# Subject-wise channel mixing with residual: stores and loads in turn in one DMA queue, 16 slots instead of 8

## The chip, the core and the metric

The kernel runs on one NeuronCore of a Trainium2 chip. The metric is the device time of one execution in microseconds (us); three runs of the kernel before lie between 334.43 and 335.13 us, with a median of 335.07 us. A difference of 0.2% is 0.67 us.

## What is computed

`x` is 128 samples of 128 channels by 1024 times, in float32 (67.1 MB). Each sample has a subject number from 0 to 7, and each subject a 128x128 weight matrix. The output is the sample plus its channels mixed by its subject's matrix:

```python
w = weights[subjects]                       # (128, 128, 128)
out = jnp.einsum('bct,bcd->bdt', x, w)      # one 128x128 by 128x1024 product per sample
x = x + out
```

Every byte of `x` is read once and every byte of the output is written once: 67.1 MB each way, and 0.5 MB of weights.

## The kernel before, in words

A tile is two samples (GROUP = 2): 128 partitions (channels) of 2 x 1024 floats, which is 1 MB. There are 64 tiles. They pass through `ring`, a buffer in SBUF with 8 slots (SLOTS) of one tile each; a turn is one pass over the slots, so there are 8 turns. The first turn and the last are written out, those between are a loop.

Each engine runs its own program, and semaphores tie them together:

- SyncE (SP) issues the loads, L82. From the second turn on it first waits, per slot, for the store that empties it (`stored[s]`, L76). The very last tile is loaded as two halves (L80).
- GpSimd (POOL) waits for the subject numbers and for the whole weight table (L91, L92). For each sample it reads the subject number (L97) and copies that subject's matrix from `table` to one of four buffers `selected` (L102).
- TensorE (PE) waits for the tile's load and for the selected matrix, and makes the product of the sample into one of four PSUM buffers (L126). The trace shows four matmul records for each sample, thus eight for a tile.
- VectorE (DVE) adds the product to the tile in its slot (L142) and counts `sum_ready`.
- ScalarE (ACT) computes nothing. It issues the loads of the subject numbers (L151) and of the table (L152), and then the stores: when both samples of a tile are summed it stores the tile (L168), the last tile in two halves (L163).

So loads travel in one DMA queue (SP's, q1 in the trace) and the table and all stores in another (ACT's, q10). Both queues are served by the same 16 DMA engines. What orders them is that a slot's load waits for the slot's store, and a store for the slot's sums.

Of the kernel before, what the change touches and what calls it, by code (L numbers as in the profile page):

```python
# [1 line left out]

# [5 lines left out]
I32 = mybir.dt.int32  # L24

GROUP = 2
SLOTS = 8
BUFS = 4
BANK = 512
DMA = 16  # L30


def subject_mix_kernel(nc: bass.Bass, x: bass.AP, subjects: bass.AP, weights: bass.AP, out: bass.AP):
    samples, channels, times = x.shape
    n_subjects, _, mixed = weights.shape
    per_turn = SLOTS * GROUP
    turns = samples // per_turn
    banks = times // BANK
    assert turns * per_turn == samples and banks * BANK == times and channels == mixed == 128
    assert per_turn % BUFS == 0  # L40
    uses = per_turn // BUFS


    x_view = x.rearrange("b c t -> c b t")
    out_view = out.rearrange("b d t -> d b t")

    with ExitStack() as ctx:
        def sem(name):
            return ctx.enter_context(nc.semaphore(name))

        ring = ctx.enter_context(nc.sbuf_tensor("ring", [channels, SLOTS, GROUP, times], F32))
        table = ctx.enter_context(nc.sbuf_tensor("table", [channels, n_subjects * mixed], F32))
        subject_row = ctx.enter_context(nc.sbuf_tensor("subject_row", [1, samples], I32))
        selected = ctx.enter_context(nc.sbuf_tensor("selected", [channels, BUFS, mixed], F32))
        products = ctx.enter_context(nc.psum_tensor("products", [mixed, BUFS, times], F32))


        subjects_loaded = sem("subjects_loaded")
        table_loaded = sem("table_loaded")
        x_loaded = [sem(f"x_loaded{s}") for s in range(SLOTS)]  # L60
        single_loaded = [sem(f"single_loaded{g}") for g in range(GROUP)]
        stored = [sem(f"stored{s}") for s in range(SLOTS)]
        weights_selected = sem("weights_selected")

        product_ready = [sem(f"product_ready{k}") for k in range(BUFS)]
        sum_ready = [sem(f"sum_ready{k}") for k in range(BUFS)]

        block = ctx.enter_context(nc.Block())

        @block.sync  # L70
        def _(sp):
            def go_round(turn, first=False, last=False):
                for s in range(SLOTS):
                    if not first:

                        sp.wait_ge(stored[s], turn * DMA)  # L76
                    start = turn * per_turn + s * GROUP
                    if last and s == SLOTS - 1:
                        for g in range(GROUP):
                            sp.dma_start(ring[:, s, g], x_view[:, start + g, :]).then_inc(single_loaded[g], DMA)  # L80
                        continue
                    sp.dma_start(ring[:, s], x_view[:, bass.ds(start, GROUP), :]).then_inc(x_loaded[s], DMA)  # L82

            go_round(0, first=True)
            with sp.Fori(1, turns - 1) as turn:
                go_round(turn)
            go_round(turns - 1, last=True)

        @block.gpsimd
        def _(pool):  # L90
            pool.wait_ge(subjects_loaded, DMA)  # L91
            pool.wait_ge(table_loaded, DMA)  # L92

            def go_round(turn, first=False):
                for j in range(per_turn):
                    k = j % BUFS
                    subject = pool.value_load(subject_row[0:1, bass.ds(turn * per_turn + j, 1)],  # L97
                                              min_val=0, max_val=n_subjects - 1)
                    if not first or j >= BUFS:

                        pool.wait_ge(product_ready[k], turn * uses + j // BUFS)
                    nc.gpsimd.tensor_copy(selected[:, k, :],  # L102
                                          table[:, bass.ds(subject * mixed, mixed)]).then_inc(weights_selected, 1)

            go_round(0, first=True)
            with pool.Fori(1, turns) as turn:
                go_round(turn)

        @block.tensor
        def _(pe):  # L110
            def go_round(turn, first=False, last=False):
                for j in range(per_turn):
                    s, g, k = j // GROUP, j % GROUP, j % BUFS

                    if last and s == SLOTS - 1:
                        pe.wait_ge(single_loaded[g], DMA)
                    elif g == 0:
                        pe.wait_ge(x_loaded[s], turn * DMA + DMA)

                    pe.wait_ge(weights_selected, turn * per_turn + j + 1)  # L120
                    if not first or j >= BUFS:

                        pe.wait_ge(sum_ready[k], turn * uses + j // BUFS)
                    for n in range(banks):
                        cols = slice(n * BANK, (n + 1) * BANK)
                        product = nc.tensor.matmul(products[:, k, cols], selected[:, k, :], ring[:, s, g, cols],  # L126
                                                   start=True, stop=True)
                    product.then_inc(product_ready[k], 1)

            go_round(0, first=True)  # L130
            with pe.Fori(1, turns - 1) as turn:
                go_round(turn)
            go_round(turns - 1, last=True)

        @block.vector
        def _(dve):
            def go_round(turn, first=False):
                for j in range(per_turn):
                    s, g, k = j // GROUP, j % GROUP, j % BUFS

                    dve.wait_ge(product_ready[k], turn * uses + j // BUFS + 1)
                    nc.vector.tensor_tensor(ring[:, s, g, :], products[:, k, :], ring[:, s, g, :],  # L142
                                            ALU.add).then_inc(sum_ready[k], 1)

            go_round(0, first=True)
            with dve.Fori(1, turns) as turn:
                go_round(turn)

        @block.scalar
        def _(act):  # L150
            act.dma_start(subject_row[:], subjects.rearrange("(a b) -> a b", a=1)).then_inc(subjects_loaded, DMA)  # L151
            act.dma_start(table[:].rearrange("c (n d) -> c n d", n=n_subjects),  # L152
                          weights.rearrange("n c d -> c n d")).then_inc(table_loaded, DMA)

            def go_round(turn, first=False, last=False):
                for s in range(SLOTS):
                    start = turn * per_turn + s * GROUP
                    if last and s == SLOTS - 1:
                        for g in range(GROUP):

                            j = s * GROUP + g
                            act.wait_ge(sum_ready[j % BUFS], turn * uses + j // BUFS + 1)
                            act.dma_start(out_view[:, start + g, :], ring[:, s, g]).then_inc(stored[s], DMA)  # L163
                        continue

                    for j in range(s * GROUP, (s + 1) * GROUP):
                        act.wait_ge(sum_ready[j % BUFS], turn * uses + j // BUFS + 1)  # L167
                    act.dma_start(out_view[:, bass.ds(start, GROUP), :], ring[:, s]).then_inc(stored[s], DMA)  # L168

            go_round(0, first=True)  # L170
            with act.Fori(1, turns - 1) as turn:
                go_round(turn)
            go_round(turns - 1, last=True)

            for s in range(SLOTS - 1):
                act.wait_ge(stored[s], turns * DMA)
            act.wait_ge(stored[SLOTS - 1], (turns - 1 + GROUP) * DMA)


# [14 lines left out]
```

## Time and profile before

| | |
|---|---|
| median of three runs | 335.07 us |
| lowest, highest | 334.43, 335.13 us |
| span of the profiled execution, first to last instruction | 330.9 us |
| rate over the span | 407 GB/s (134.78 MB) |
| PE busy | 234.2 us, 71% |
| DVE busy | 156.8 us, 47% |
| POOL busy | 37.8 us, 11% |
| granted TensorE clock, mean | 0.988 |

The span goes from the first to the last instruction of the program. The page gives no time of the profiled execution besides its span; the median of the runs is 4.2 us longer than the span (335.07 - 330.86), which is taken here for what lies around it. Busy shares are means over the whole span, and the first 60 us look different from the rest: there PE works without a pause.

### The profile page before, as it was taken

The page shows a single profiled execution, that of the slowest core. Times are in us where ns is not written, and L with a number is a line of the kernel's source. Part 1 is how long each engine was busy: PE and PEld are TensorE (multiplying, and loading weights), DVE is VectorE, ACT ScalarE, POOL GpSimd, SP SyncE. Part 2 cuts the span into 40 slices and gives each one's busy share as a digit, 9 for nine tenths or more (in the row PEclk, how much of TensorE's full clock was granted, in tenths as well). Part 3 has the DMA queues.
Part 4 walks back from the last instruction along what each step waited for, and adds up shares of the span by engine and source line. Part 5 has one row for each costly group of instructions (what it writes and reads, how often), then busy time and mean ns, then how long its engine had stood idle before and what let it go on. Part 6 is the DMA issues. An engine that isn't in the chain of part 4 may idle for free.

```text
span 330.9 us, 2706 instructions
## 1 busy us (share of the span) xinstructions
PE 234.2 (71%) x512; PEld 93.6 (28%) x512; DVE 156.8 (47%) x128; POOL 37.8 (11%) x133
## 2 busy tenths in 40 slices
PE   0069999976876866866866866866867767767750
PEld 0024444332332332322322322322322322322310
DVE  0017777745445445445445445445445445445450
POOL 0011111101111111111111111111111111111000
PEclk9999999999999999999999999999999999999995
DMA  7996999999999999999999999999999999999997
GB/s 272 391 409 245 364 420 419 419 421 423 420 420 420 420 421 421 421 422 420 420 420 420 421 422 422 420 420 420 419 421 421 423 421 420 420 420 421 421 421 308
DMA packets 35893, 134.78 MB, mean 407 GB/s; under 512 B 2097, under 2 KB 3122, under 8 KB 35890
## 3 DMA queue, kind: packets, MB, share of 16 engines
q10 hardware_dynamic: 18466, 67.64, 50.3%
q1 hardware_dynamic: 17424, 67.11, 50.0%
q8 instruction: 1, 0.02, 0.0%
q14 instruction: 2, 0.02, 0.0%
HBM read 67.63 MB, written 67.11 MB: 407 GB/s over the span
## 4 chain that ended last, share of the span: by engine, by line
DMA 75%; PE 17%; DVE 3%; issue 1%; ACTq 0%; POOLq 0%; SPq 0%; POOL 0%
DMA out<-ring 46%; DMA ring<-x 24%; PE products L126 17%; DMA table<-weights 5%; DVE ring L142 3%; POOLq L97 0%; ACTq L151 0%; ACTq L168 0%; SPq L82 0%; ACTq L167 0%; POOLq L102 0%; POOLq L92 0%; POOL selected L102 0%
## 5 line engine op out<-in xcount | busy, mean ns | idle before, releaser
L126 PE MATMUL products<-ring,selected 128*128 128x512 f32 x512 | 234.2, 604 | 84.6 <-DMA ring<-x 65.1
L142 DVE TENSOR_TENSOR ring<-products,ring 128x1024 f32<-128x1024 f32 x128 | 156.8, 1225 | 163.2 <-PE products L126 163.2
L126 PEld LDWEIGHTS products<-ring,selected 128*128 128x128 f32 x512 | 93.6, 191 | 224.3 <-issue 162.5
L102 POOL COPY selected<-table 128x128 f32 x128 | 37.6, 294 | 272.7 <-PE products L126 253.0
L185 POOL MEMSET const-float32-0.0<- 128x1 f32 x1 | 0.1, 98 | 0.1
L185 POOL MEMSET const-bfloat16-1.0<- 128x1 bf16 x1 | 0.1, 101 | 0.0
L185 POOL MEMSET const-uint8-127<- 128x1 uint8 x1 | 0.1, 101 | 0.0
L185 POOL MEMSET const-float32-1.0<- 128x1 f32 x1 | 0.1, 98 | 0.0
L185 POOL BASE_LOAD x1 | 0.0, 17 | 0.2 <-issue 0.2
## 6 DMA issues: line engine op xcount, KB each, us to landing
ring<-x SPq DMA_DIRECT2D x63, 1024.0 KB, 11.4
out<-ring ACTq DMA_DIRECT2D x63, 1024.0 KB, 22.9
ring<-x SPq DMA_DIRECT2D x2, 512.0 KB, 10.7
out<-ring ACTq DMA_DIRECT2D x2, 512.0 KB, 10.3
table<-weights ACTq DMA_DIRECT2D x1, 512.0 KB, 16.7
subject_row<-subjects ACTq DMA_DIRECT2D x1, 0.5 KB
```

What stands on the lines that cost most here:

```text
L102: nc.gpsimd.tensor_copy(selected[:, k, :], table[:, bass.ds(subject * mixed, mixed)]).then_inc(weights_selected, 1)
L126: product = nc.tensor.matmul(products[:, k, cols], selected[:, k, :], ring[:, s, g, cols], start=True, stop=True)
L142: nc.vector.tensor_tensor(ring[:, s, g, :], products[:, k, :], ring[:, s, g, :], ALU.add).then_inc(sum_ready[k], 1)
L185: nc = bacc.Bacc("TRN2", target_bir_lowering=False, num_devices=1)
```

## The change

All data transfers but the 0.5 KB of subject numbers are now issued by SP, in one queue. SP issues the table first, then loads of the first eight tiles. From there on it takes turns: it waits until tile t is summed, issues the store of tile t, waits (from tile 8 on) until the store of tile t-8 has landed, whose slot it needs, and issues the load of tile t+8. The ring has 16 slots, so there are 4 turns of 16. The last tile is loaded and stored whole. ACT issues the subject numbers and nothing else. What PE, DVE and POOL do with a tile stays as it was.

```diff
-SLOTS = 8
+SLOTS = 16
+AHEAD = 8
...
         @block.sync
         def _(sp):
+            def load(tile, s):
+                sp.dma_start(ring[:, s], x_view[:, bass.ds(tile * GROUP, GROUP), :]).then_inc(x_loaded[s], DMA)
+
+            sp.dma_start(table[:].rearrange("c (n d) -> c n d", n=n_subjects),
+                         weights.rearrange("n c d -> c n d")).then_inc(table_loaded, DMA)
+            for tile in range(AHEAD):
+                load(tile, tile)
+
             def go_round(turn, first=False, last=False):
                 for s in range(SLOTS):
-                    if not first:
+                    tile = turn * SLOTS + s
+                    for j in range(s * GROUP, (s + 1) * GROUP):
+                        sp.wait_ge(sum_ready[j % BUFS], turn * uses + j // BUFS + 1)
+                    sp.dma_start(out_view[:, bass.ds(tile * GROUP, GROUP), :], ring[:, s]).then_inc(stored[s], DMA)
+                    if last and s >= SLOTS - AHEAD:
+                        continue
+                    into = (s + AHEAD) % SLOTS
+                    if s >= SLOTS - AHEAD:
 
-                        sp.wait_ge(stored[s], turn * DMA)
-                    start = turn * per_turn + s * GROUP
-                    if last and s == SLOTS - 1:
-                        for g in range(GROUP):
-                            sp.dma_start(ring[:, s, g], x_view[:, start + g, :]).then_inc(single_loaded[g], DMA)
-                        continue
-                    sp.dma_start(ring[:, s], x_view[:, bass.ds(start, GROUP), :]).then_inc(x_loaded[s], DMA)
+                        sp.wait_ge(stored[into], turn * DMA + DMA)
+                    elif not first:
+                        sp.wait_ge(stored[into], turn * DMA)
+                    sp.dma_start(ring[:, into], x_view[:, bass.ds((tile + AHEAD) * GROUP, GROUP), :]
+                                 ).then_inc(x_loaded[into], DMA)
...
         @block.scalar
         def _(act):
             act.dma_start(subject_row[:], subjects.rearrange("(a b) -> a b", a=1)).then_inc(subjects_loaded, DMA)
-            act.dma_start(table[:].rearrange("c (n d) -> c n d", n=n_subjects),
-                          weights.rearrange("n c d -> c n d")).then_inc(table_loaded, DMA)
-
-            def go_round(turn, first=False, last=False):
...
```

At the head of the program, SP before: eight loads, and in the loop a load for each slot behind the wait for its store (`stored0` is slot 0's).

```order
L82 DMA ring<-x 128x2x1024 x8
L85 UNCONDITIONAL_BRANCH
L85 ISA
L82 ISA [waits stored0]
L82 DMA ring<-x 128x2x1024
L82 ISA [waits stored1]
L82 DMA ring<-x 128x2x1024
```

At the same place ACT before: the table, then the stores, each behind the two sums of its tile.

```order
L149 UNCONDITIONAL_BRANCH [waits barrier_Pool_Activation_PE_DVE_SP_release]
L151 DMA subject_row<-subjects 1x128
L152 DMA table<-weights 128x8x128
L168 DMA out<-ring 128x2x1024 [waits sum_ready1,sum_ready0]
L168 DMA out<-ring 128x2x1024 [waits sum_ready3,sum_ready2]
```

SP now, at the head of the program and where the first slots are used again:

```order
L59 DMA table<-weights 128x8x128
L57 DMA ring<-x 128x2x1024 x8
L69 DMA out<-ring 128x2x1024 [waits sum_ready1,sum_ready0]
L78 DMA ring<-x 128x2x1024
L69 DMA out<-ring 128x2x1024 [waits sum_ready3,sum_ready2]
L78 DMA ring<-x 128x2x1024
...
L69 DMA out<-ring 128x2x1024 [waits sum_ready1,sum_ready0]
L78 DMA ring<-x 128x2x1024 [waits stored0]
```

The table has moved from ACT to the front of SP, and each store has come between two loads; the first eight of those loads wait for no store. At the end of the program SP before (above) and now (below):

```order
L82 DMA ring<-x 128x2x1024 [waits stored5]
L82 DMA ring<-x 128x2x1024 [waits stored6]
L80 DMA ring<-x 128x1024 [waits stored7]
L80 DMA ring<-x 128x1024
L47 UNCONDITIONAL_BRANCH
```

```order
L69 DMA out<-ring 128x2x1024 [waits sum_ready1,sum_ready0]
L78 DMA ring<-x 128x2x1024 [waits stored14]
L69 DMA out<-ring 128x2x1024 [waits sum_ready3,sum_ready2]
L78 DMA ring<-x 128x2x1024 [waits stored15]
L69 DMA out<-ring 128x2x1024 [waits sum_ready1,sum_ready0]
L69 DMA out<-ring 128x2x1024 [waits sum_ready3,sum_ready2]
```

Behind the last load there now stand eight stores in the same queue (the last two rows, four times over).

## Rows read from the trace of the kernel before

**Rows 1.** The page: span, busy time, 40 slices of the span.
```profile
span 330.9 us, 2706 instructions
PE 234.2 (71%) x512; PEld 93.6 (28%) x512; DVE 156.8 (47%) x128; POOL 37.8 (11%) x133
DMA  7996999999999999999999999999999999999997
GB/s 272 391 409 245 364 420 419 419 421 423 420 420 420 420 421 421 421 422 420 420 420 420 421 422 422 420 420 420 419 421 421 423 421 420 420 420 421 421 421 308
```
**Rows 2.** Windows: start:end and us, busy us of each engine, PEclk, DMA share, GB/s.
```profile
0.00:3.00 3.00, 0.00 (x0) 0.00 (x0) 0.00 (x0) 0.22 (x5) 1.00 0.28 30
6.00:17.00 11.00, 0.00 (x0) 0.00 (x0) 0.00 (x0) 0.00 (x0) 1.00 1.04 394
18.00:24.00 6.00, 4.51 (x7) 2.08 (x8) 0.97 (x1) 1.46 (x5) 1.00 1.03 412
25.00:27.00 2.00, 2.00 (x6) 0.93 (x5) 1.51 (x2) 0.46 (x2) 1.00 0.05 18
29.00:31.00 2.00, 2.00 (x6) 0.80 (x6) 1.51 (x2) 0.29 (x1) 1.00 0.60 240
31.00:34.00 3.00, 3.00 (x9) 1.33 (x8) 2.01 (x3) 0.59 (x2) 1.00 0.99 288
34.00:37.00 3.00, 3.00 (x9) 1.33 (x8) 2.02 (x3) 0.33 (x2) 1.00 1.01 332
42.00:60.00 18.00, 18.00 (x43) 7.98 (x42) 13.07 (x11) 3.23 (x11) 1.00 1.03 421
60.00:300.00 240.00, 178.78 (x390) 69.84 (x388) 119.12 (x98) 28.51 (x97) 1.00 1.02 421
317.00:328.00 11.00, 1.73 (x4) 0.42 (x3) 2.45 (x2) 0.00 (x0) 0.77 1.02 419
328.00:331.00 3.00, 0.00 (x0) 0.00 (x0) 0.00 (x0) 0.00 (x0) 0.50 0.23 92
```
**Rows 3.** The chain that ended last, in order of time: start, us, what.
```profile
1.38 16.66 DMA table<-weights
...
72.30 3.71 PE products L126 x8
...
76.04 1.23 DVE ring L142
...
77.48 22.84 DMA out<-ring
...
100.48 11.35 DMA ring<-x
```
**Rows 4.** Timeline around the first tiles: start, us, engine, line, what.
```profile
19.49 25.82 PE L126 MATMUL products<-ring,selected 128*128 128x512 f32 x56 [19.49 <-POOL selected L102]
...
26.06 17.54 ACTq L168 DMA_DIRECT2D out<-ring  x6
```
**Rows 5.** DMA queues from 18 to 24 us, packets, MB, share of 16 engines.
```profile
q1 hardware_dynamic: 635, 2.47, 103.1%
```
**Rows 6.** DMA queues from 317 to 328 us.
```profile
q10 hardware_dynamic: 1206, 4.61, 102.1%
```
**Rows 7.** DMA queues from 6 to 17 us.
```profile
q10 hardware_dynamic: 982, 0.50, 15.7%
```
**Rows 8.** DMA queues from 31 to 34 us, and from 34 to 37 us below.
```profile
q10 hardware_dynamic: 206, 0.79, 93.7%
q1 hardware_dynamic: 17, 0.07, 5.6%
...
q1 hardware_dynamic: 240, 0.96, 98.0%
q10 hardware_dynamic: 13, 0.04, 3.0%
```
**Rows 9.** Line 82, SP's loads: ns to issue, min/median/max; then times to landing.
```profile
L82 SPq DMA_DIRECT2D ring<-x x63: 367/373/2648, 0.8 to 299.6; - x63
...
DMA to landing us min/median/max: 5.3/11.4/20.3
```

29 lines of the change are left out of this document (5 added, 24 removed).

## The prediction, made before the changed kernel ran

> **What bounds the kernel now.** I read the page's slices first. The DMA row stands at 9 in all but a few slices, and the rate is flat at 420 GB/s from slice 6 to slice 39, while PE is busy for 71% and DVE for 47% of the span [rows 1]. So the data transfers bound the kernel, and its time is the bytes by the rate plus the stretches in which the rate is not reached. The windows give those [rows 2]. The flat rate is 421 GB/s (60 to 300 us, DMA share 1.02), and at that rate the page's 134.78 MB take 320.1 us. The span is 330.9 us, so 10.8 us are lost. A window loses its length times (1 - rate/421):
>
> - 0 to 3 us, start: 3 x (1 - 30/421) = 2.8 us
> - 6 to 17 us, the table's small packets among the loads: 11 x (1 - 394/421) = 0.7 us
> - 25 to 27 us, almost no transfer (18 GB/s): 1.9 us
> - 29 to 31 us (240 GB/s, share 0.60): 0.9 us
> - 31 to 34 and 34 to 37 us (288 and 332 GB/s, but share 0.99 and 1.01): 0.95 + 0.63 = 1.6 us
> - 328 to 331 us, the end: 2.3 us
>
> That is 10.2 of the 10.8 us; the rest is spread thinly over 18 to 24 us (412 GB/s) and windows I don't list. The chain and the timeline say why 25 to 31 us are lost. The table needs 16.66 us to land because it shares the engines with eight loads [rows 3]; PE can't start before 19.49 us, and the first store leaves at 26.06 us [rows 4]. By then all eight slots have been loaded, and no load can be issued until a store has emptied one. Behind that, PE makes tiles at 8 x 0.43 = 3.43 us each, so stores alone don't fill the engines. Later PE has a tile only every 5 us and is no limit.
>
> **The change, part by part.** The sum goes against this execution: a span of 330.9 us and 4.2 us around it, which makes 335.1, the median.
>
> 1. *Table first.* The table no longer shares the engines with loads. Its 982 packets between 6 and 17 us took 15.7% of 16 engines for 11 us, which is 28 ns each [rows 7]. All 1024 alone: 64 on each engine, 1.8 us, where 0.52 MB at 421 GB/s take 1.25 us. The loss is then 0.55 us against 0.7 us before: no change. That these packets take 28 ns with no large packet among them isn't shown by any row. The upper bound is the time of a 4 KB packet, 4096 B at 421/16 GB/s = 156 ns, which would make it 10 us and cost 8.2 us. I take 28 ns, the only row with such packets.
>
> 2. *The gap from 25 to 31 us goes: -2.8 us.* With the table landed at about 5 us and the first load 2.5 us behind it, PE starts at about 8.5 us. The first store left 6.57 us after PE's start (26.06 - 19.49) [rows 4], so now at about 15 us. The table and eight loads keep the queue busy until 2.8 + 1.8 + 8 x 2.5 = 24.6 us. The first store and ninth load stand in the queue almost 10 us before they are needed, and the ninth load waits for no store, as there are 16 slots. From there PE yields a pair of work (store and load, 5 us) every 3.43 us, so the queue grows.
>
> 3. *The slow stretch from 31 to 37 us: -1.6 us.* Here the engines were not idle; packets took longer. First q10 moves nearly everything (93.7% of the engines), then q1 (98.0%) [rows 8], although the other queue also had transfers issued: it is the first meeting of a queue of stores and a queue of loads. With one queue there is no such meeting. Bounds: all 1.6 us go, or all stay. I take it as gone, since the stretch comes once, and 42 to 60 us run at 421.
>
> 4. *One queue instead of two: +1.5 us.* In the flat stretch packets of two queues take turns. A queue alone appears twice: stores alone from 317 to 328 us at 419 GB/s (1206 packets, all q10) and loads alone from 18 to 24 us at 412 GB/s (all q1) [rows 2, 5, 6]. At 419 the 134.78 MB take 321.7 us, 1.5 us more than at 421. I use this for loads too: a load burst is now 1 MB long (2.5 us), with stores on both sides. The bounds are 421 (0 us) and 412 for the loads; the latter adds 67.1 MB x (1/0.412 - 1/0.419) = 2.7 us (GB/s written in MB per us).
>
> 5. *SP's waits.* SP now waits for the sums of tile t, and behind that wait stands the load of t+8. From the landing of load t it takes 0.2 + 3.71 + 1.23 = 5.2 us until both samples are summed [rows 3]. Between load t and store t the queue holds 14 transfers, 35 us of work, so SP comes 30 us early. If the queue takes only about 8 transfers (before, with eight loads issued, one issue took 2648 ns against a median of 373 [rows 9]), SP is held by the queue and not by the sums, with about 12 us to spare still. The added wait for store t-8 is for a transfer that stands directly ahead of load t and has long landed. Two issues cost 0.75 us of each 5 us. All this costs nothing; the cover is the queue's backlog. ACT waits no more and nobody waited for it otherwise.
>
> 6. *The end.* Before, the last tile came in halves, and the engines ran at 419 until 328 us. Now eight stores stand behind the last load, 20 us of work, against 5.2 us for the last sums. The last store goes without a gap. The end's 2.3 us stay. PE's idle time before the end costs nothing.
>
> Sum: 330.9 - 2.8 - 1.6 + 1.5 = 328.0 us of span, and with 4.2 us around it **332.2 us**, 0.9% less than before.
>
> **The rivals.**
>
> *A. Loads in bursts run at the load-only rate.* Nothing else changes, the loads run at 412 GB/s: 332.2 + 2.7 = 334.9 us, no change. For it: the six-microsecond stretch of loads alone, the only long one in the trace. Against it: with one queue the engines need not be in step, some may store while others load. I give it one in six. The Trainium skill ("DMA: Bandwidth & Descriptors", section "iDMA fabric — 4 AXI ports for 8 engines, asymmetric across TPBs") has a load stream issued from SP, in 1 MiB transfers of 4 KiB rows and with nothing beside it, at 408.7 GB/s; an estimate from that page's figure is 4.0 us above my sum, 336.2 us. By that rule, the trace agrees within 1% in its stretch of loads alone (412 GB/s), and shows no stretch of loads in bursts between stores.
>
> *B. Each change of direction costs.* In one ring a load stands behind a store and has to read from HBM while the store's writes drain. From the first store to the last load there are 113 changes of direction. The gain of my sum, 2.9 us, is used up if each costs 26 ns, a sixth of a packet's 156 ns. For it: when stores and loads first met, an engine's packets took up to half as long again (288 against 421 GB/s at a full share) [rows 2, 8], which lost 1.6 us over two or three changes; at that price for all, some 0.5 us each, the kernel would take 390 us. Against it: in the flat stretch each engine has both directions under way at all times at 421 GB/s, but with a queue for each. Priced at one packet for each of the 56 loads behind a store, 56 x 0.156 = 8.7 us: 340.9 us, slower. A price of a third of that gives 335.1 us.
>
> *C. The rate doesn't fall.* If the 419 of stores alone is only the unevenness of the end, item 4 is nothing and the time is 330.7 us, or 330.1 if the small losses between 17 and 42 us that I don't list go as well.
>
> *D. The table is slow alone.* At twice to three times 28 ns, the added cost is 1.8 to 3.6 us, which puts it at 334 to 336 us. That the change doesn't do what it says (SP held at a wait while the queue runs dry) I give almost nothing, since the cover in item 5 is more than twice the need.
>
> **How the numbers follow.** A measurement of this kernel tells about 0.2% (0.67 us) from no change, so faster is below 334.4 and slower above 335.7. My forecast with C on its lower side, 330.0 to 334: 0.55. Rival A, 334 to 335.6: 0.17. Rival D: 0.06, half of it within 0.2%. Rival B: 0.22, of which half lies below 339. The predicted time is the forecast's, 332.2. The range 330.0 to 339.0 leaves out about 0.11 above and less than 0.05 below. Faster: 0.55 + 0.03 + a part of A = 0.60; same: 0.16; slower: 0.24.
>
> **What would show it.** In the changed kernel's profile: q1 carries nearly all bytes; PE starts near 8.5 us and the first store is issued near 15 us (item 2); no window between 20 and 45 us falls below 410 GB/s (items 2, 3); the rate from 60 to 300 us is 419 (item 4; 416 for A, 421 for C, 410 or less for B); loads take over 30 us to land and nobody waits for them longer; the table lands at about 5 us (8 or later for D); the last window looks as before. I am wrong if the flat rate is below 415, or if SP waits for sums while the DMA share drops.

## The result: 5.5 us faster, below the predicted range

The changed kernel takes 329.21 us (median of four runs, 328.76 to 329.42), the kernel before 334.75 us with one more run added to its three. The ratio is 0.984, with a 95% interval from 0.982 to 0.987. The prediction said 332.2 us and a range from 330.0: the direction was right, the gain was nearly twice the forecast, and the time lies 0.8 us under the range.

The page of the changed kernel, the lines that answer to [rows 1]; in the 40 slices the dip near slice 4 is gone:

```profile
span 327.7 us, 2553 instructions
DMA  7999999999999999999999999999999999999995
GB/s 259 410 409 419 422 420 420 419 421 421 420 422 420 421 419 421 420 420 422 421 422 420 421 422 421 421 422 421 422 421 420 422 421 420 422 421 421 422 420 243
...
q1 hardware_dynamic: 35856, 134.75, 100.6%
```

Its windows, against [rows 2] (start:end and us, busy us of each engine, PEclk, DMA share, GB/s):

```profile
3.00:6.00 3.00, 0.00 (x0) 0.00 (x0) 0.00 (x0) 0.00 (x0) 1.00 1.09 375
6.00:17.00 11.00, 9.24 (x16) 4.10 (x17) 3.67 (x3) 2.05 (x7) 1.00 1.03 411
...
25.00:27.00 2.00, 2.00 (x6) 0.84 (x5) 1.51 (x2) 0.29 (x1) 1.00 1.01 416
27.00:29.00 2.00, 2.00 (x6) 0.95 (x5) 1.40 (x2) 0.29 (x1) 1.00 1.03 418
29.00:31.00 2.00, 2.00 (x6) 0.86 (x5) 1.23 (x1) 0.29 (x1) 1.00 1.03 420
31.00:34.00 3.00, 3.00 (x9) 1.33 (x8) 2.41 (x2) 0.59 (x2) 1.00 1.02 419
34.00:37.00 3.00, 3.00 (x9) 1.33 (x8) 2.02 (x3) 0.59 (x2) 1.00 1.03 423
...
60.00:300.00 240.00, 176.29 (x384) 69.06 (x384) 117.26 (x96) 28.15 (x96) 1.00 1.02 421
...
317.00:325.00 8.00, 0.00 (x0) 0.00 (x0) 0.00 (x0) 0.00 (x0) 0.50 0.90 371
325.00:328.00 3.00, 0.00 (x0) 0.00 (x0) 0.00 (x0) 0.00 (x0) 0.50 0.06 23
```

Three things are to be seen. From 25 to 37 us the rate never falls below 416 GB/s, where before four of the five windows had 18, 240, 288 and 332. The flat stretch runs at 421 GB/s with one queue, exactly as with two. And the end is worse than before: from 317 us on the engines thin out.

The timeline of the first tile (start, us, engine, line, what), against [rows 4]:

```profile
7.76 8.71 PE L123 MATMUL products<-ring,selected 128*128 128x512 f32 x14 [7.76 <-DMA ring<-x]
...
15.24 0.39 SPq L69 DMA_DIRECT2D out<-ring  x1
```

### The profile page after: what moved, and what is told of

It is laid out like the page before. It is cut to its first block, busy times and chain, and to the rows that moved or that the text cites. A ratio compares the mean times of both kernels' runs of the same rounds, so it can differ in the third digit from the quotient of the medians.

```text
span 327.7 us, 2553 instructions
## 1 busy us (share of the span) xinstructions
PE 236.7 (72%) x512; PEld 94.7 (29%) x512; DVE 156.8 (48%) x128; POOL 37.8 (12%) x133
## 4 chain that ended last, share of the span: by engine, by line
SPq 70%; PE 12%; DMA 8%; issue 4%; DVE 1%
SPq L69 41%; SPq L78 29%; PE products L123 12%; DMA ring<-x 8%; DVE ring L138 1%; SPq L68 0%; SPq L59 0%; SPq L82 0%; SPq L75 0%
## 5 line engine op out<-in xcount | busy, mean ns | idle before, releaser
L123 PE MATMUL products<-ring,selected 128*128 128x512 f32 x512 | 236.7, 610 | 74.7 <-DMA ring<-x 74.7
L123 PEld LDWEIGHTS products<-ring,selected 128*128 128x128 f32 x512 | 94.7, 193 | 215.9 <-issue 157.1
## 6 DMA issues: line engine op xcount, KB each, us to landing
ring<-x SPq DMA_DIRECT2D x64, 1024.0 KB, 18.1
```

## Where the time went, and what was to be tested

In spans, the profiled executions differ by 330.9 - 327.7 = 3.2 us, and the prediction's 328.0 us of span was close to 327.7. In times the kernels differ by 5.5 us. So most of the miss is not in the difference of these two spans. My theory after the result, the gap theory: what gains is that transfers are always issued between 25 us and the first stores, and neither the number of queues nor the turn-taking matters. Its rival, the queue theory: one queue of stores and loads in turn is itself what gains. Besides these, two things were unexplained: time minus span, and the slow packets from 31 to 37 us [rows 8].

### One part at a time

*e1: two queues and 8 slots stay; only the table moves to the front of SyncE's queue.*

```diff
+            sp.dma_start(table[:].rearrange("c (n d) -> c n d", n=n_subjects),
+                         weights.rearrange("n c d -> c n d")).then_inc(table_loaded, DMA)
             go_round(0, first=True)
...
-            act.dma_start(table[:].rearrange("c (n d) -> c n d", n=n_subjects),
-                          weights.rearrange("n c d -> c n d")).then_inc(table_loaded, DMA)
```

> The kernel before with one edit: SyncE issues the table ahead of its loads (8 slots and two queues stay). Gap theory (the 4.4 us lost from 25 to 37 us are what the change gains, whichever queue carries what): PE starts near 8.5 us, the first store leaves near 15 us, and slots come free before the eighth load has landed, so that the gap closes in part: 331 to 332 us. Queue theory (what gains is that loads and stores share one queue): the gap from 25 to 31 us moves but the rest stays, within 1 us of before. If part of the gain lies outside the span (after the last transfer, on ScalarE), the time minus the span stays as in the runs of before.

Measured: 328.88 us (328.44 to 329.33), ratio to the kernel before 0.984 (0.981 to 0.987). Two of its windows: PE and DVE are at work long before 25 us, stores leave while the eight loads are still under way, and the rate doesn't drop, although the ring has 8 slots.

```profile
17.00:25.00 8.00, 8.00 (x20) 3.61 (x19) 5.81 (x5) 1.48 (x5) 1.00 1.02 405
25.00:27.00 2.00, 2.00 (x6) 0.86 (x5) 1.51 (x2) 0.29 (x1) 1.00 1.02 420
```

I had expected only part of the gap to close. All of it did. The queue theory falls: no single queue and no turn-taking is in this kernel.

*e2: two queues and the late table stay; 16 slots.*

```diff
-SLOTS = 8
+SLOTS = 16
```

> The kernel before with 16 slots and nothing else; the table still shares the engines with the loads and PE starts near 19.5 us or later. Gap theory: sixteen loads keep the engines busy until the stores come, no window from 25 to 31 us falls under 380 GB/s, 330.5 to 331.5 us. Queue theory: within 1 us of before. The stretch in which packets take up to twice as long when the first stores meet loads (1.6 us of loss) should stay if it comes from two queues meeting, and go if it came from the empty queue.

Measured: 329.14 us (328.94 to 329.21), ratio 0.985 (0.982 to 0.988). This is 1.4 us less than the lower expectation. The table is as late as before and PE starts at 19 us, and yet the gain is there; and stores meet loads of another queue without a slow stretch:

```profile
25.00:27.00 2.00, 2.00 (x6) 0.95 (x5) 1.27 (x2) 0.30 (x1) 1.00 1.01 406
...
31.00:34.00 3.00, 3.00 (x8) 1.33 (x7) 2.02 (x3) 0.35 (x2) 1.00 1.04 427
```

*e3: both edits together, still two queues.*

> Table first on SyncE and 16 slots, but stores still leave from ScalarE in their own queue: everything of the change but the single queue. Gap theory: the same as the changed kernel, 329.2 us (within 0.5). Queue theory: at least 2 us slower than the changed kernel. If the 2.5 us by which time minus span differs between the kernels (4.2 against 1.7 us) come from the engine that waits for the stores at the end, this kernel keeps 4.2 and takes about 331.5 us.

Measured: 328.71 us (328.56 to 328.86), ratio 0.984 (0.981 to 0.986). Either edit closes the gap, and both together give no more than one.

*e4: the changed kernel with the table back on ScalarE.*

```diff
-            sp.dma_start(table[:].rearrange("c (n d) -> c n d", n=n_subjects),
-                         weights.rearrange("n c d -> c n d")).then_inc(table_loaded, DMA)
...
+            act.dma_start(table[:].rearrange("c (n d) -> c n d", n=n_subjects),
+                          weights.rearrange("n c d -> c n d")).then_inc(table_loaded, DMA)
```

> The changed kernel, but with the table issued by ScalarE as before: it shares the engines with eight loads and lands near 17 us, PE starts near 19 us and the first store leaves near 26 us, after the eighth load has landed at about 25 us. Gap theory: about 1 to 2 us of idle transfer come back, and PE makes pairs of work every 3.4 us from then on, so the rest of the gap stays closed: 330 to 331.5 us. If the table's place doesn't matter: 329.2 us.

Measured: 333.65 us (333.0 to 334.29), ratio 0.998 (0.996 to 1.000). One queue, 16 slots and the turn-taking without the early table are worth next to nothing, and nothing at all in the span: its ten spans (331.3 to 332.6 us) are those of the kernel before, and what is left of the gain lies outside the span. Both my numbers were too low, by 2.2 and 4.4 us, and the windows show what I had missed:

```profile
25.00:27.00 2.00, 2.00 (x6) 0.95 (x5) 1.51 (x2) 0.57 (x2) 1.00 0.00 0
27.00:29.00 2.00, 2.00 (x6) 0.82 (x5) 1.51 (x2) 0.30 (x1) 1.00 1.01 373
29.00:31.00 2.00, 2.00 (x6) 0.89 (x5) 1.51 (x2) 0.29 (x1) 1.00 1.07 246
31.00:34.00 3.00, 3.00 (x8) 1.33 (x7) 2.02 (x3) 0.59 (x2) 1.00 0.95 341
```

The engines stand still for about 2 us, and after that they are busy (shares 1.01, 1.07, 0.95) at 373, 246 and 341 GB/s: another 1.6 us lost, by the formula of the prediction. There is only one queue of stores and loads here. So the slow stretch of [rows 8] is no matter of two queues meeting. In this kernel it follows idle time.

*g1: e4 with AHEAD = 12.*

```diff
-AHEAD = 8
+AHEAD = 12
```

> The one-queue kernel with the late table (e4, 333.65 us) and AHEAD = 12 instead of 8: twelve loads and the table keep the engines busy until about 35 us, while the first store still leaves near 26 us. Theory that the time is lost because nothing is issued between 25 us and the first store: no window from 25 to 37 us under 380 GB/s and 329.0 to 329.7 us, although the table is as late as before. If the late table itself costs the time: it stays at 333 us or more.

Measured: 329.75 us (329.60 to 329.84), ratio 0.986 (0.984 to 0.987). With twelve loads issued instead of eight the late table costs nothing much, as expected: 3.9 us back from one number. The lowest window between 25 and 37 us has 403 GB/s. What counts is whether work is queued when the first store leaves.

### What an idle moment costs

If the slow stretch follows idle time, it must move with it. The next three runs put the idle moment elsewhere.

*f6: the changed kernel with AHEAD = 3.*

> The changed kernel with AHEAD = 3: the queue holds the table and three loads, empties at about 12.3 us and gets the first store at about 15.2 us, some 3 us of idle transfer long before 25 us; from then on two pairs (10 us) stand between a load and its store, against 5.2 us needed. Theory that engines which have stood idle start slowly: idle time plus at least 1 us more in windows after 16 us in which the DMA share is near 1 but the rate is under 400 GB/s, thus 333 to 334.5 us. Theory that the slow stretch belongs to the time (30 to 37 us) or to the first meeting of stores and loads: 329.2 plus the idle 3 us only, 332.2 to 332.7 us, and no such windows near 18 us.

Measured: 337.84, 340.52, 344.00 and 354.27 us; in the last two the mean granted clock of PE was 0.962 and 0.925, in the first two 0.988 and 0.981. The profiled execution is the one of 340.52 us, with a span of 338.8 us. Its start did what the idle theory says:

```profile
12.00:13.00 1.00, 1.00 (x4) 0.49 (x3) 0.62 (x1) 0.00 (x0) 1.00 0.01 4
13.00:16.00 3.00, 3.00 (x8) 1.33 (x7) 2.10 (x2) 0.59 (x2) 1.00 0.13 53
16.00:18.00 2.00, 2.00 (x6) 0.83 (x5) 1.51 (x2) 0.29 (x1) 1.00 1.03 348
18.00:20.00 2.00, 2.00 (x6) 0.69 (x4) 1.29 (x2) 0.29 (x1) 1.00 0.94 225
20.00:22.00 2.00, 0.24 (x1) 0.00 (x0) 1.23 (x1) 0.29 (x1) 1.00 1.01 307
22.00:24.00 2.00, 0.70 (x2) 0.46 (x3) 0.00 (x0) 0.00 (x0) 1.00 1.03 422
```

Idle from 12 to 16 us (3.6 us lost), then six microseconds at shares near 1 with 348, 225 and 307 GB/s, which lose 0.35 + 0.93 + 0.54 = 1.8 us, then 422. It happened at 16 to 22 us, not at 31 to 37. The time came out 3 us or more above the expectation (6 us in the profiled execution), and two more windows show the rest:

```profile
60.00:100.00 40.00, 29.06 (x58) 11.34 (x57) 17.51 (x15) 4.37 (x15) 0.92 1.02 400
100.00:140.00 40.00, 29.13 (x61) 11.61 (x60) 19.21 (x16) 4.48 (x16) 0.95 1.00 385
```

They lose 2.0 + 3.4 = 5.4 us, and PE's granted clock fell below 1 in them. The chain has PE at 3.71 us for the tile at 63.20 us, and at 5.41 us for the one at 79.67, after 2.81 us without work; from 80 to 82 us the granted clock is 0.52, near the lower of its two levels (1.2 of 2.4 GHz):

```profile
63.20 3.71 PE products L123 x8
...
79.67 5.41 PE products L123 x8
...
80.00:82.00 2.00, 2.00 (x3) 0.67 (x2) 0.00 (x0) 0.00 (x0) 0.52 1.01 416
```

In this execution the losses add up: 327.7 + 3.6 + 1.8 + 5.4 = 338.5 us, against a span of 338.8. With two pairs (10 us) between a load and its store, a tile that takes 1.7 us longer is still in time by my sum (landing to store 6.9 us). But SP issued stores at 73.22 and 78.20 us and the next only at 86.41 us, so the cover is thinner than counted; which part of it was counted wrong stays open.

The windows behind that late store correct the idle theory:

```profile
86.00:88.00 2.00, 2.00 (x6) 0.76 (x4) 1.51 (x2) 0.30 (x1) 1.00 0.95 387
88.00:90.00 2.00, 0.75 (x3) 0.25 (x2) 1.27 (x2) 0.29 (x1) 1.00 1.00 330
90.00:92.00 2.00, 2.00 (x5) 0.81 (x5) 0.23 (x1) 0.10 (x1) 1.00 1.08 268
92.00:94.00 2.00, 1.45 (x4) 0.38 (x2) 1.51 (x2) 0.49 (x2) 1.00 0.92 307
```

These six microseconds from 88 to 94 us look like those from 16 to 22 us and cost the same, 0.43 + 0.73 + 0.54 = 1.7 us, but the engines had hardly paused before them (share 0.95 from 86 to 88 us). So idle time is not needed for the slow stretch.

*e6: the changed kernel with AHEAD = 4.*

> The changed kernel with AHEAD = 4 and 16 slots: the same queue as the run with 8 slots and AHEAD = 4, so the same span within 0.5 us, with time minus span 1.75 us. Three pairs (15 us) stand between a load and its store. The theory that a thin queue lets PE idle, lose its clock and then hold up the stores says it happens with AHEAD = 3 only: here no window from 60 to 300 us under 415 GB/s.

Measured: 331.66 us (330.95 to 332.44), ratio 0.992 (0.990 to 0.995); the flat stretch stays at 421 GB/s.

```profile
14.00:16.00 2.00, 2.00 (x6) 0.93 (x5) 1.47 (x2) 0.29 (x1) 1.00 0.52 207
16.00:18.00 2.00, 2.00 (x6) 0.81 (x6) 1.22 (x1) 0.29 (x1) 1.00 1.03 307
18.00:20.00 2.00, 2.00 (x6) 0.93 (x5) 1.33 (x2) 0.29 (x1) 1.00 0.98 299
20.00:22.00 2.00, 2.00 (x6) 0.92 (x5) 1.51 (x2) 0.56 (x2) 1.00 0.98 338
```

An idle moment of about 1 us (share 0.52 in a window of 2 us) is followed by the same slow six microseconds: 0.54 + 0.58 + 0.39 = 1.5 us. So the price of the slow stretch does not depend on how long the engines stood: 1.5 us after 1 us, 1.8 us after 3.6 us, 1.6 us after 2 us in e4, and 1.7 us at 88 us in f6, after next to none.

*e5: the same with 8 slots.*

> The changed kernel with 8 slots and AHEAD = 4. Four loads and the table keep the engines busy until about 14.8 us, the first store leaves near 15 us: an idle time of under 1 us. Theory that the restart after idle time costs: 0.7 us idle plus up to 1.8 us, thus 329.9 to 332 us. If only long idle times are followed by slow packets: 329.5 to 330 us. Time minus span: 2.4 us, if that belongs to programs with 8 slots (all four so far) and not to the engine that ends or the queue.

Measured: 331.38 us (330.86 to 332.50), ratio 0.991 (0.989 to 0.994), with the same slow windows (297, 285 and 350 GB/s from 16 to 22 us). Again the number of slots does nothing.

Nor do engines that have stood still always start slowly. In the kernel before, the first store leaves alone, with no load behind it, after 2 us of idle engines, and it runs at 406 and 397 GB/s (first and second row); the first load is issued at 30.24 us, behind the second store, and the slow microseconds come after that (third row):

```profile
27.00:28.00 1.00, 1.00 (x4) 0.40 (x3) 0.69 (x1) 0.00 (x0) 1.00 0.99 406
28.00:29.00 1.00, 1.00 (x4) 0.52 (x3) 0.82 (x1) 0.29 (x1) 1.00 1.01 397
...
32.00:33.00 1.00, 1.00 (x4) 0.41 (x3) 0.83 (x1) 0.03 (x1) 1.00 1.07 262
```

What the slow stretches of the kernel before and of e4, e5, e6 and f6 have in common is a queue that has run empty, or nearly, and then a store with a load issued behind it and little else to do. A change from storing to loading that all 16 engines make at the same time would fit that, and would also fit that a full queue has no such stretch; no run took it apart, so it is argued, not shown.

### Time outside the span

The four runs of e1 take 2.4 us more than their spans, those of e2, e3 and e4 1.7 to 1.8 us, and 44 further runs of the kernel before 2.4 to 2.5 us. My first guess was the engine that waits for the stores at the end.

*f4: the kernel before with its last waits on SyncE.*

```diff
-            for s in range(SLOTS - 1):
-                act.wait_ge(stored[s], turns * DMA)
-            act.wait_ge(stored[SLOTS - 1], (turns - 1 + GROUP) * DMA)
...
+            for s in range(SLOTS - 1):
+                sp.wait_ge(stored[s], turns * DMA)
+            sp.wait_ge(stored[SLOTS - 1], (turns - 1 + GROUP) * DMA)
```

> The kernel before with one edit: the last waits for the eight slots' stores stand at the end of SyncE's program, not ScalarE's. In the runs so far a kernel whose ScalarE waits for the stores takes 2.4 us more than its span, one whose SyncE waits takes 1.7 us. If the engine that ends last makes that, time minus span falls from 2.4 to 1.7 us and the time by 0.7 us against the kernel before; if it's the queue that carries the stores (ScalarE still issues them), it stays at 2.4.

Measured: 334.72 us (333.54 to 335.48), ratio 1.001 (0.999 to 1.003); time minus span stays at 2.4 to 2.5 us.

*f5: the changed kernel with its last waits on ScalarE.*

> The changed kernel with its last waits for the stores on ScalarE, which otherwise only loads the subject numbers. If the engine that ends last makes the difference outside the span, time minus span rises from 1.75 to 2.4 us, and the time from 329.2 to 329.9 us; if it's the queue that carries the stores, both stay.

Measured: 328.95 us (328.55 to 329.14); time minus span stays at 1.7 us. So it is neither the engine that ends, nor the queue that carries the stores (e2 has them on ScalarE and 1.7 us). It goes with the program: before, e1, f3, f4 and h3 have 2.4, e5 has 2.2, and all with 16 slots have 1.7 to 1.8. The trace gives one hint. In the kernel before, a transfer of instructions falls behind the end of the span (DMA queues from 331 to 334 us):

```profile
q14 instruction: 1, 0.01, 1.2%
```

The changed kernel has no transfer at all behind its last instruction. Over all sixteen traces the fetch is there in the six whose programs have 2.2 to 2.5 us (before, e1, e5, f3, f4, h3) and missing in the ten with 1.7 to 1.8. That it is the 0.7 us fits, but no run took it away by itself; it stays argued.

### Is there a price of the single queue, and a kernel that beats both

*f3: table first and last waits on SyncE, two queues, 8 slots.*

> The kernel before with the table first on SyncE and the last waits on SyncE, 8 slots and two queues: the two parts that seem to matter and nothing else. 328.9 us less 0.7 us if the ending engine matters: 328.2 us, a microsecond faster than the changed kernel. If it doesn't: 328.9 us.

Measured: 328.52 us (328.25 to 329.19). It seemed the fastest, so three kernels were timed side by side.

> The changed kernel once more, beside two two-queue kernels on the same chip: 329.2 us, span 327.4 us.

> The same as e3: all of the change but the single queue. It was 0.5 us faster than the changed kernel, in another set of runs. If two queues are truly a little better: 328.7 us, 0.3 to 0.6 us under the changed kernel in this set. If that was the chip: within 0.2 us of it. Rival A or B of the prediction in small (a single queue loses something at changes of direction) would show as a rate under 420 GB/s in the changed kernel's flat stretch; the loss may also be the end, where a single engine finishes late.

> The same as f3: table first on SyncE, 8 slots, two queues. 328.5 us: with half the ring it is at least as fast as the changed kernel, although its time minus span is 0.7 us larger.

Measured: h1, the changed kernel, 328.93 us (328.82 to 329.11), ratio to the kernel before 0.984 (0.982 to 0.986); h2, two queues with 16 slots, 328.81 us (328.63 to 329.37); h3, two queues with 8 slots, 329.37 us (328.53 to 329.63). The ranges overlap. The single queue costs nothing that can be measured in the time, nor does it bring anything, and no version clearly beats the changed kernel. The one with the table moved (e1) reaches it with half the ring.

## Why the prediction was off, point by point

**The time around the span: the step that failed.** The prediction's last step added 4.2 us to the span it had worked out. It set the profiled span of 330.9 us against the median of 335.07 us and called the difference of 4.2 us "what lies around it". Forty-four further runs of the kernel before have spans from 330.8 to 333.3 us, median 331.9, and take 2.4 to 2.5 us beyond them. The profiled execution had one of the shortest spans, so 1.8 of the 4.2 us were no time around the span but a difference between executions. With 2.4 us the same sum gives 330.4 us, and with the 0.7 us by which the time outside the span also fell, 329.7 us. That is 2.5 of the 3.0 us by which I missed. Of the rest, 0.3 us are the span (327.7 against 328.0), and by 0.2 us the profiled execution of the changed kernel is longer than its median.

**The span of 328.0 us was right by luck.** Two terms of the sum were wrong by more than its total was: item 4 put +1.5 us where nothing was lost, and item 6 put nothing where 1.2 us were. They cancel. Without item 4's 1.5 us alone the forecast would have been case C's 330.7 us, within the range.

**The kernel before varies where its gap is.** f4 is the kernel before but for its last waits, and its profiled execution has a span of 332.5 us. Its windows against [rows 2]:

```profile
25.00:27.00 2.00, 2.00 (x6) 0.95 (x5) 1.22 (x1) 0.29 (x1) 1.00 0.00 0
27.00:29.00 2.00, 2.00 (x6) 0.85 (x5) 1.22 (x1) 0.29 (x1) 1.00 0.56 227
29.00:31.00 2.00, 2.00 (x6) 0.85 (x5) 1.41 (x2) 0.34 (x2) 1.00 0.76 297
31.00:34.00 3.00, 3.00 (x8) 1.33 (x7) 2.27 (x2) 0.54 (x2) 1.00 0.92 307
34.00:37.00 3.00, 3.00 (x8) 1.33 (x7) 2.25 (x2) 0.59 (x2) 1.00 1.01 328
37.00:42.00 5.00, 5.00 (x13) 2.28 (x12) 3.52 (x4) 0.88 (x3) 1.00 0.99 388
```

From 25 to 42 us it loses 2.0 + 0.9 + 0.6 + 0.8 + 0.7 + 0.4 = 5.4 us, where the profiled execution before lost 4.5 us in the same stretch; at its end it loses 2.9 us against 2.3. That makes most of the 1.6 us between the two spans. A change that closes such a gap gains more in the median than in a lucky profile. The changed kernel's four spans lie within 0.7 us.

**Item 1, the table: right.** Landed near 5 us (median time to landing 4.3 us, issued at 0.8 us). From 3 to 6 us the rate is 375 GB/s, a loss of 0.3 us, which is a little less than my 0.55.

**Item 2, the gap: right.** PE starts at 7.76 us (8.5 said), the first store leaves at 15.24 us (15 said), no idle time until the end. The 2.8 us are gained.

**Item 3, the slow stretch: right size, wrong cause.** The 1.6 us went. But I had put them down to the first meeting of two queues. e4, e5, e6 and f6 show the stretch within one queue, e2 shows two queues meeting without it, and f6 moves it to another time and has it a second time without an idle moment. It comes when the queue has run empty or thin, and the change keeps the queue full. For rival B, which took its price from this stretch, what counts is the flat stretch: there the direction changes with every transfer, at 421 GB/s. If a change of direction costs anything, it does so only when the queue is thin.

**Item 4, one queue: +1.5 us expected, 0 measured.** The flat stretch has 421 GB/s. The 419 GB/s of stores alone [rows 6] and the 412 of loads alone in the first 24 us [rows 5] weren't limits of a queue with both in turn. This was case C. Rivals A (416) and B (410 or less) did not occur. The load stream that the Trainium skill ("DMA: Bandwidth & Descriptors", section "iDMA fabric — 4 AXI ports for 8 engines, asymmetric across TPBs") has at 408.7 GB/s is near the changed kernel's own loads before the first store, 411 GB/s from 6 to 17 us. Loads in bursts of 1 MB between stores are not held to it: with them the trace shows 421.

**Item 5, SP's waits: right.** The issue of a load takes a median of 2.3 us now, against 373 ns [rows 9], and a load lands 18 us after it:

```profile
L78 SPq DMA_DIRECT2D ring<-x x56: 377/2283/2908, 15.7 to 288.1; - x56
...
DMA to landing us min/median/max: 6.4/18.1/19.2
```

So the queue takes about 18.1/2.5 = 7 transfers and SP is held by the queue, as the second case of that item had it. My mark "over 30 us to land" belonged to the first case and was wrong.

**Item 6, the end: no change expected, +1.2 us between the two profiles.** After the bulk has gone, some engines are late. Single microseconds of the changed kernel:

```profile
323.00:324.00 1.00, 0.00 (x0) 0.00 (x0) 0.00 (x0) 0.00 (x0) 0.50 0.77 315
324.00:325.00 1.00, 0.00 (x0) 0.00 (x0) 0.00 (x0) 0.00 (x0) 0.50 0.28 115
325.00:326.00 1.00, 0.00 (x0) 0.00 (x0) 0.00 (x0) 0.00 (x0) 0.50 0.12 49
326.00:327.00 1.00, 0.00 (x0) 0.00 (x0) 0.00 (x0) 0.00 (x0) 0.50 0.05 20
```

From 317 us to its end the changed kernel loses 0.95 + 2.5 = 3.5 us, the kernel before 2.3 us from 328 us on. A share of 0.05 to 0.12 is one or two of 16 engines at work. Two-queue versions of the early table thin out too (e1: 357 GB/s from 317 to 325 us). But by the same formula, from 317 us to the end of the span, the eight traces with two queues lose 2.2 to 3.1 us, and seven with one queue (all but f6) 3.1 to 3.6. So up to 1 us may go with the one-queue kernels, which also load and store their last tile whole, where the others have two halves; no run took these apart. The changed kernel also fetches instructions more often, eight packets against three (queues q8 and q14), but e1 has three and loses 3.0 us.

So in spans: -2.8 - 1.6 + 0 + 1.2 and about -0.2 for a smoother start make 330.9 - 3.4 = 327.5 us, against the measured 327.7.

## What to carry to other kernels

When the transfers bound a kernel, look for the moment at which nothing is issued, and ask what makes it: here the eight loads issued at once were done before the first store, and each of three edits closes that gap alone: an early table, more slots for loads that wait only for slots, or, in one queue, loads further ahead. Count a moment at which the DMA queues run empty dearer than it is long: here the six microseconds behind it cost 1.5 to 1.8 us more. And compare a profiled span with the spans of other executions before you take the rest of the median for time around it.

## What was unexpected of the hardware

When the queue has run empty or nearly so and work then comes as a store with a load behind it, the DMA engines show busy shares near 1 for about six microseconds and move only 225 to 350 GB/s in most of that time, which costs 1.5 to 1.8 us (e4, e5, e6, f6, and the kernel before). It happens after idle engines (1 to 4 us) and, in f6 at 88 us, after a share of 0.95. It does not happen to a lone store behind idle engines (406 and 397 GB/s). Where the queue stays full, stores and loads take turns, in one queue or in two, at 421 GB/s. What makes the packets slow was not tested.
